# The rows of three norms: split into f16 halves by token and transposed by DMA, in a Mamba-2 block with MLP and routed LoRA

## The reference, cut to what matters

```python
x = hidden_states                                  # 8 x 256 x 512
x = x + layernorm(attn(layernorm(x)))              # attn: Mamba-2 and MLP, below
x = x + layernorm(ffn(layernorm(x)))               # ffn: linear and routed LoRA

def attn(h):
    t = rmsnorm(h, ln1_w)
    zxbcdt = t @ w_in.T                            # z 512, xs 128, B 128, C 512, dt 4
    xBC = silu(causal_conv4(xs, B, C) + conv_b)
    dt = softplus(dt + dt_bias)                    # per token and head
    Y = chunked_scan(xBC, dt, -exp(A_log))         # 2 chunks of 128 tokens, 4 heads of 128
    y = (Y + D * xs) * silu(z)
    h = h + y @ w_out.T
    t = rmsnorm(h, ln2_w)
    return h + (silu(t @ gate_w.T) * (t @ up_w.T)) @ down_w.T      # 1792 wide

def ffn(t):
    e = argmax(t @ gate_w.T + expert_bias)         # 1 of 4
    return t @ W_up.T + (t @ lora_A[e].T) @ lora_B[e].T            # rank 8
```

## Time and profile before

| | |
|---|---|
| median of 3 runs | 866.3 us (863.62 to 866.99) |
| the profiled execution | 866.66 us, with a span of 864.7 us from its first to its last instruction |
| mean granted TensorE clock | 0.969 of full speed |
| TensorE, VectorE, ScalarE, GpSimd busy | 92%, 57%, 39%, 23% of the span |
| a step of the loop | 95.3 us (383.60 to 478.93 us from one `hn` transposition to that of the next step) |

### The profile page before, as it was taken

The page is one execution under the profiler, slowest core; times in us unless marked ns, Lnnn a source line. Parts: engine busy times, 40 slices in busy tenths (PEclk is TensorE's granted clock), DMA queues, the critical chain, the costliest instruction groups (busy, mean ns, idle before and its releaser), DMA issues.

```text
span 864.7 us, 15301 instructions
## 1 busy us (share of the span) xinstructions
PE 793.6 (92%) x5726; PEld 555.5 (64%) x5726; DVE 492.0 (57%) x1142; ACT 338.0 (39%) x625; POOL 197.7 (23%) x232
## 2 busy tenths in 40 slices
PE   3876897979999999999999999999999999999945
PEld 3644574547765786567766786668756785577632
DVE  6777744677544665357643765457534754455343
ACT  2713555632651345323642355224632365122211
POOL 3723546401320122102410123012210123000000
PEclk9999899999999999999999999999999999999986
DMA  9920000000001000020002000020002000000010
GB/s 336 386 98 2 1 1 25 2 24 2 1 1 60 15 1 2 0 74 0 0 0 73 0 0 0 0 73 0 0 0 73 0 0 0 30 20 1 4 47 25
DMA packets 15557, 29.70 MB, mean 34 GB/s; under 512 B 1312, under 2 KB 1440, under 8 KB 15520
## 3 DMA queue, kind: packets, MB, share of 16 engines
q1 hardware_dynamic: 15520, 29.21, 9.6%
HBM read 25.01 MB, written 4.19 MB: 34 GB/s over the span
## 4 chain that ended last, share of the span: by engine, by line
PE 62%; issue 16%; DVE 12%; POOL 6%; ACT 4%; DMA 0%; DVEq 0%; SPq 0%; POOLq 0%; ACTq 0%
PE gu L1221 23%; PE wa L1221 18%; PE acc L1221 13%; PE wc L1221 6%; POOL y L441 3%; PE wa L1244 2%; DVE xbc L930 1%; POOL ra L425 1%; DVE weights L870 1%; ACT weights L568 1%; DVE hn L899 1%; DVE hn L907 1%; DVE stats_a L885 1%; DVE weights L1033 1%; DVE h2t L1010 1%
## 5 line engine op out<-in xcount | busy, mean ns | idle before, releaser
L1221 PE MATMUL gu<-h2t,weights 128*128 128x256 f16 x2688 | 313.6, 274 | 0.4 <-issue 0.4
L1221 PEld LDWEIGHTS gu<-h2t,weights 128*128 128x128 f16 x2688 | 261.4, 98 | 50.6 <-issue 16.2
L1221 PE MATMUL acc<-weights,act 128*128 128x512 f16 x672 | 166.3, 384 | 14.2 <-DVE act L1021 14.2
L1016 DVE SCALAR_TENSOR_TENSOR sg<-gu,bound,sg 128x256 f32<-128x256 f32 x112 | 53.6, 479 | 111.6 <-ACT sg L668 111.2
L1221 PEld LDWEIGHTS acc<-weights,act 128*128 128x128 f16 x672 | 65.1, 99 | 73.2 <-DVE act L1021 16.6
L668 ACT ACTIVATE sg<-gu,scale_inv 128x256 f32<-128x256 f32 x112 | 53.0, 474 | 144.5 <-PE gu L1221 144.4
L1221 PE MATMUL wa<-ht,weights 128*128 128x256 f16 x912 | 107.3, 277 | 0.0
L1221 PEld LDWEIGHTS wa<-ht,weights 128*128 128x128 f16 x912 | 90.8, 100 | 18.1 <-issue 0.5
L678 ACT ACTIVATE act<-sg 128x256 f16<-128x256 f32 x112 | 46.8, 418 | 141.4 <-DVE sg L1016 140.6
L930 DVE SCALAR_TENSOR_TENSOR xbc<-conv_pad,conv_ws,xbc 128x256 f32<-128x256 f32 x144 | 69.5, 524 | 30.8 <-ACT conv_pad L603 21.5
L1021 DVE TENSOR_TENSOR act<-sg,act 128x256 f16<-128x256 f32 x112 | 50.9, 454 | 55.0 <-ACT act L678 55.0
(11 more groups left out here) (194 smaller groups left out, 935.8 us busy)
## 6 DMA issues: line engine op xcount, KB each, us to landing
xa<-in_x SPq DMA_DIRECT2D x8, 512.0 KB, 3.5
weights<-in_x SPq DMA_DIRECT2D x8, 512.0 KB, 4.1
out_x<-h SPq DMA_DIRECT2D x16, 256.0 KB, 2.1
weights<-in_w_in SPq DMA_DIRECT2D x5, 512.0 KB, 6.8
weights<-in_w_gate SPq DMA_DIRECT2D x2, 1024.0 KB, 14.3
weights<-in_w_up SPq DMA_DIRECT2D x2, 1024.0 KB, 14.8
weights<-in_w_down SPq DMA_DIRECT2D x2, 1024.0 KB, 12.9
weights<-in_w_gate SPq DMA_DIRECT2D x2, 768.0 KB, 12.2
```

What stands on the lines that cost most here:

```text
L1016: nc.vector.scalar_tensor_tensor(sg[:, f % 2], GU[f % 2][:, SEQ:2 * SEQ], up_to_act, sg[:, f % 2], ALU.mult, ALU.mult).then_inc(sem("prod_ ...
L1221: return nc.tensor.matmul(dst, left, right, start=start, stop=stop)
```

## The change

The split is moved ahead of the transposition. ScalarE writes the upper half of each row (token) of `hn` or `h3`, in f16 and by tile of 128 tokens, VectorE the lower half, both from and to SBUF, into `rows_a` (the memory of `ra`) or `rows_c` (that of `dec`), a row being 1024 f16 values. SP then issues one DMA transpose for each tile of 128 tokens, from 128 x 1024 to eight blocks of 128 x 128 in `ht`, `h2t` or `h3t`. TensorE's f32 transposes go, except `ht` of group 0, which stays as it was. The new work stands in block 0 (ht), 12 (h2t) and 3 (h3t). On SP each transpose stands in the one queue, behind its waits. `prev` takes the wait function instead of the engine; calls that differ in that alone are left out here, as are the removed forms that are like the ones shown.

```diff
+        rows_a, rows_c = [t[:].rearrange("p t h q -> p (t h q)").bitcast(F16)
+                          .rearrange("p (t s d) -> p t s d", t=TILES, s=2) for t in (ra, dec)]
...
-        def prev(g, per, k, eng, s):
+        def prev(g, per, k, wait, s):
...
+            def wait_apart(s, value):                      # SP
+                sp.wait_ge(s, value)
+                sp.sem_inc(sem("sp_waited"), 1)
+            def transposed(dst, rows, j, done):
+                sp.dma_start_transpose(dst[:, :, :, j * P:(j + 1) * P].rearrange("p s k q -> p (s k) q"),
+                                       rows[:, j].rearrange("p s d -> p (s d)")).then_inc(done, 16)
+            def a_t1(g):
+                prev(g, 2, 2, wait_apart, sem("z_ps_ready"))
+                prev(g, 1, 1, wait_apart, sem("dt_ps_ready"))
+                for j in range(TILES):
+                    wait_apart(sem("hn_split"), g * 2 + j - 1)
+                    transposed(ht, rows_a, j, ht_loaded)
+            def a_t2(g):
+                prev(g, FBLK, FBLK, wait_apart, sem("gu_ready"))
+                for j in range(TILES):
+                    wait_apart(sem("h2_split"), g * 2 + j + 1)
+                    transposed(h2t, rows_a, j, h2t_loaded)
+            def c_t3(g):
+                prev(g, 2, 2, wait_apart, sem("u_ps_ready"))
+                for j in range(TILES):
+                    wait_apart(sem("h3_split"), g * 2 + j + 1)
+                    transposed(h3t, rows_c, j, h3t_loaded)
...
+            def step(a, b, c):
+                if a is not None:
+                    a_x(a)
+                    a_t1(a)
+                if c is not None:
+                    c_x(c)
+                    c_t3(c)
+                    c_store(c)
+                if a is not None:
+                    a_t2(a)
+
+            a_t2(0)
...
+            def a_hi1(g):                                  # ScalarE; a_hi2 and c_hi3 are alike
+                eng.wait_ge(h2t_loaded, g * 32)
+                for j in range(TILES):
+                    eng.wait_ge(sem("hn_ready"), g * 2 + j + 1)
+                    nc.scalar.activation(rows_a[:, j, 0], hn[:, j], ACT.Copy).then_inc(sem("hn_hi"), 1)
...
-            A_AT = {1: lambda g: a_t1(g), 2: lambda g: a_conv(g, 0),
+            A_AT = {0: lambda g: a_hi1(g), 2: lambda g: a_conv(g, 0),
...
-                    10: lambda g: a_sumsq(g, 0), 11: lambda g: a_sumsq(g, 1), 13: lambda g: a_t2(g)}
-            C_AT = {4: lambda g: c_t3(g, 0), 5: lambda g: c_t3(g, 1), 7: lambda g: c_zt(g),
+                    10: lambda g: a_sumsq(g, 0), 11: lambda g: a_sumsq(g, 1), 12: lambda g: a_hi2(g)}
+            C_AT = {3: lambda g: c_hi3(g), 7: lambda g: c_zt(g),
...
+            def a_lo1(g):                                  # VectorE; a_lo2 and c_lo3 are alike
+                for j in range(TILES):
+                    dve.wait_ge(sem("hn_hi"), g * 2 + j - 1)
+                    nc.vector.tensor_tensor(rows_a[:, j, 1], hn[:, j], rows_a[:, j, 0], ALU.subtract)\
+                        .then_inc(sem("hn_split"), 1)
...
+            A_AT = {0: lambda g: (a_center(g), a_norm(g), a_lo1(g)), 2: lambda g: a_conv(g, 0),
...
-                    12: lambda g: (a_h2(g, 0), a_h2(g, 1))}
+                    12: lambda g: (a_h2(g, 0), a_h2(g, 1), a_lo2(g))}
...
-            C_AT = {1: lambda g: c_x1(g), 2: lambda g: c_stats2(g), 3: lambda g: c_h3(g), 4: lambda g: c_t3(g, 0),
-                    5: lambda g: c_t3(g, 1), 6: lambda g: c_route(g), 9: lambda g: c_stats3(g),
+            C_AT = {0: lambda g: c_stats1(g), 1: lambda g: c_x1(g), 2: lambda g: c_stats2(g),
+                    3: lambda g: (c_h3(g), c_lo3(g)), 6: lambda g: c_route(g), 9: lambda g: c_stats3(g),
...
             def a_in(g, b):                                # TensorE
-                pe.wait_ge(sem("ht_ready"), g * 2 + 2)
-                if b == 0:
-                    prev(g, 2, 2, pe, sem("h2t_ready"))
+                if head(g):
+                    pe.wait_ge(sem("ht_ready"), 2)
+                else:
+                    pe.wait_ge(ht_loaded, g * 32)
+                prev(g, 2, 2, pe.wait_ge, sem("h1_ready"))
...
             def b_gu(g, f):
                 if f == 0:
-                    pe.wait_ge(sem("h2t_ready"), g * 2 + 1)
+                    pe.wait_ge(h2t_loaded, g * 32 + 32)
...
-            def c_t3(g, b):
-                if b == 0:
-                    pe.wait_ge(sem("h3_ready"), g * 2 + 2)
-                    prev(g, 2, 2, pe, sem("u_ready"))
-                elif alone(g):
-                    pe.wait_ge(sem("prod_ready"), g * FBLK + FBLK)
-                else:
-                    pe.wait_ge(sem("h3t_ready"), g * 2 + 1)
-                transposed(h3, h3t_bank(g, b), b, sem("h3t_ps_ready"))
...
             def c_logits(g):
-                pe.wait_ge(sem("h3t_ready"), g * 2 + 2)
+                pe.wait_ge(h3t_loaded, g * 32 + 32)
+                prev(g, 2, 2, pe.wait_ge, sem("u_ready"))
```

More of the change, by code:

```diff
@@ L634, in a_exp @@
                 if n == 0:
[L635 removed]
+                    prev(g, 2, 2, eng.wait_ge, sem("y_ps_ready"))
+                    if not isinstance(g, int) or g >= 2:
+                        eng.wait_ge(h3t_loaded, g * 32 - 32)
                 if n == 2 and not head(g):
@@ L1129, in step @@
                     chain_c.group(c)
-                if a is not None and not (isinstance(a, int) and a == 0):
+                if a is not None:
                     chain_a.group(a)
@@ L1385, in b_gu @@
                         wait_split(pe, [u])
[L1386 to L1391 removed]
+                    last = split_product(GU[f % 2][:, m * SEQ:(m + 1) * SEQ],
+                                         [weight(u, k) for k in range(KB)], [tokens(h2t, k) for k in range(KB)])
                 last.then_inc(sem("gu_ready"), 1)
```

152 lines of the change are left out of this document (61 added, 91 removed).

## The result

The changed kernel takes 895.5 us (median of 4 runs, 893.58 to 897.41) against 866.64 us (4 runs, 863.62 to 871.22) on the same chip: ratio 1.032, 95% interval 1.0284 to 1.0356. It is 29 us slower. A second measurement on another chip gave 894.65 us, ratio 1.0307 (1.0275 to 1.0339). The profiled execution took 896.53 us with a span of 894.8 us, 30.1 us longer than before.

A forecast was written before the change was run, and what follows sets the result against it. TensorE, busy 92% of the span, was taken to set the pace. Terms 2.5 + 15.9 + 15.1 - 3.1 + 11.9 + 3.6 gave +45.9 on 866.66, so 912 us (885 to 960 at 50%; wider range 868 to 990).

The forecast's parts named there:

- X: Time from first issue of a DMA transpose pair to last landing: 6.1 us; h2t's wait, X - 3.45, at 6 boundaries.
- The first boundary, put at nothing: First of 7 step boundaries: no added wait for h2t, since TensorE already waited 3.91 us for VectorE there.
- Last down product late, 7 x 0.35: End of each step: VectorE's split of hn pushes the last down product back by 0.35 us.
- Act of block 1, 7 x 1.05: Second down product of each step starts 1.05 us later, because VectorE's split delays act of block 1.
- ht late, 7 x 1.1: In-projection of each step waits for ht's DMA, landing at t0+14.0 against the down product's end at t0+12.95: 1.1 us.
- t0: Start of a step's first gate/up product on TensorE, from which the prediction's times are counted; 481.11 before the change.
- h3t, 7 x -0.44: Blocks 3 to 6: DMA hidden, so half of the 0.88 us of removed transposes is saved in each of 7 groups.
- Clock, 7 x 1.7: One fall of the granted clock per step after new idle waits, 1.7 us each, 11.9 in all.
- Tail, +3.6: Last group, nothing beside it: logits wait for h3t's DMA until 849.4 instead of 845.86, +3.6 us.
- Head, 0: Program start: the first act waits for VectorE's weight preparation, hiding the transpose pair; uncovered it would cost 2.65 us.
- The sign with xa: VectorE waiting for xa over 2 us beyond old times would show the queue behind the pair was priced too low.
- The small-pieces rival: Transposes split into many small pieces, X from 9 to 13.1: longer waits at boundaries and in-projection, 959 to 1028 us; 12%.

## Why the prediction was right, and where its terms were off

The direction, the place of both new waits and the range were right; the forecast was 16 us too high. By its own steps:

- **X.** Put at 6.1 from two ends of 2.7 and 13.1; it is 4.75. Taking the middle of two ends so far apart was a guess, and it came out near by luck. The upper end had the number of pieces right (1024 and 32 more in each transpose) and their price wrong: 85.6 ns was that of the loads' and stores' packets of about 1900 bytes, and these of 256 bytes took an estimated 21 ns. What held was the formula: X - 3.45 = 1.3, and TensorE shows 1.46 released by DMA h2t (the boundary is 1.63 us longer). At 6 boundaries 15.9 us were predicted and 9.3 are there. The mechanism was right and the size off, and h2t alone by DMA confirms it as a cost of its own.
- **The first boundary, put at nothing.** Right: no wait for h2t stands there. The 0.8 us more are a lower clock over the last down product (2.74 us where before it took 1.93), and two kernels with h2t still on TensorE show the same 2.74 (ht alone by DMA, and h3t alone without the last group).
- **Last down product late, 7 x 0.35.** It is 0.08.
- **Act of block 1, 7 x 1.05.** 0.96 in the step shown, 0.91 to 1.35 over the five steps behind the first two, 0.85 with ht alone. Right.
- **ht late, 7 x 1.1, added to it.** Nothing is there, 7.7 us too many. This is X once more: the term is t0 + 7.9 + X against a down product's end at t0 + 12.95, that is X - 5.05, which is 1.1 at 6.1 and below nothing at 4.75. The delay of act was already taken off in it, so the two waits were not counted twice; a term that exists only above X = 5.05 was carried in the sum at full size. In the changed kernel the pair is issued at t0 + 8.1, and 4.75 us later TensorE is just done with the down product, even at full clock.
- **h3t, 7 x -0.44.** -0.50, shown alone.
- **Clock, 7 x 1.7.** The size is right (0.67 + 1.01 = 1.68 in the step shown, 1.68 in the run with ht alone), the count nearly so: six of the seven steps, all but the one that begins at 202.40. Filling the idle time ahead of it takes it away, filling the boundary's doesn't.
- **Tail, +3.6.** +2.1: the same formula with X = 4.75 gives 3.6 - 1.35 = 2.25.
- **Head, 0.** The first gate/up product is late by 2.9: hn is ready at 82.75, the pair is issued at 83.59, and the product follows 4.68 us later; TensorE turned the same rows in 2.58 us (79.44 to 82.02). The cover that I named, the first act, then gives it back: the first down product, which needs it, comes 6.80 us behind the first gate/up product (88.27 to 95.07) where it came 9.29 behind before (82.02 to 91.31), so that 0.4 of the 2.9 are left. The head was right at nothing.
- **The first step.** It is longer all the same, by 5.0 us from that down product to the next group's first gate/up product (107.3 against 102.3). Over all kernels profiled this stretch is 101.7 to 104.2 us with ht on TensorE and 106.6 to 108.3 with ht by DMA, so it belongs to ht; I had 2.7 us for it besides the 1.1 above, and what the rest is was not taken apart.
- **The sign with xa.** VectorE waits 2.51 us for xa at 500.60, where in the earlier trace rows it does not wait. By what I wrote, more than 2 us would mean that the queue behind the pair was priced too low. The sign was badly set, since my own times (VectorE free near 483.2, the load landed at 485.5) already hold 2.3 us; and with the wait gone (the loads first) TensorE's distances stayed.

With X = 4.75 the prediction's own formulas give 2.5 + 7.8 + 7.35 - 3.1 + 11.9 + 2.25 = 28.7 us, against 28.9 by the medians. So nearly the whole miss is X. That it fits so closely is luck: the down product's 0.35 and the seventh fall are too much, the first step too little. The small-pieces rival's 959 to 1028 comes out of its own terms as about 965 to 1022, which changes nothing.

By the gate/up products that open each group, the 30.1 us are: 6.3 to the first (2.9 of the change, most of it given back at the first down product, and 3.4 spread), 2.5 and 1.2 in the first two steps, 19.4 in the five after (3.89 each), 0.75 from there to the end.

Of the two pages weighed in the prediction, neither holds here. "Advanced Engine Details and Errata" of the Trainium skill, X-Bar Transpose (TRN2), has transposes as fast as regular DMAs; a 256 KB transpose lands in 3.3 us and a plain 256 KB store in 2.1. "VectorE: DVE Perf Modes" of the Trainium skill, The three transpose paths, has 1309 ns for one block; eight blocks hold the queue for 1.24 us and four for 1.19, so for up to eight blocks such a figure would be the price of an instruction, not of a block. A transpose of one block was not run, and sixteen blocks hold the queue for about 1.9 us.

## What to carry to other kernels

Work that a wait already covers is worth nothing when it goes, and h2t's 64 transposes stood in such a wait. ht's 56 could have given an estimated 0.7 us in each step (act of block 1 was ready at t0 + 9.8, and the product that needs it began at t0 + 10.6), but what replaced them on VectorE made act itself later. And in h2t's place came a transfer of 4.75 us with TensorE idle behind it. Only h3t, wanted 16 us after it was made, paid (0.3 to 0.4%), and the last group's, with no other work beside it, cost 2 us. When several terms of a forecast hang on one unknown time, write each as a function of it with the point at which it becomes nothing, and add them up at the low end too; at the middle value alone a term that may not exist gets its full price. And a fix of the first of several waits that end close together is handed back in part by the second and third, as three of these runs show.

## What the hardware showed that I had not expected

- A DMA transpose's time on the issuing queue hardly depends on its size up to 128x1024: 1.19 us for 128x512, 1.24 for 128x1024, about 1.9 (1.3 to 2.0 among h2t's) for 128x2048, against 0.41 for a plain 512 KB load.
- A DMA transpose is moved in one packet for each row of each 128-wide block and 32 more: 1056 for 128x1024, and by the same difference of the totals 2080 for 128x2048 and 544 for 128x512. They took an estimated 21 ns each, against 85.6 for the packets of the kernel before.
- The granted clock can fall or stay after the same idle time: 2.13 us of it, at the same place, gave 0.72 over 405 to 411 and 1.00 over 503 to 509 in one execution. A fall cost 1.68 us in the two loop steps with one of that execution, and 1.7 with the loads first.
